# Loading the stacked per-batch factors ahead of the shared factors, and opening TensorE with three rounds of ones instead of nine

## The reference, cut to what matters

```
A_eff = einsum('bn,nri->bri', gate, lora_A)
B_eff = einsum('bn,nor->bor', gate, lora_B)
y     = x @ kernel + bias + (x @ A_eff[b].T) @ B_eff[b].T + (x @ lora_A_shared.T) @ lora_B_shared.T
```

## Time and profile before

| | |
|---|---|
| time of three runs | 492.47 us in the median, 491.3 to 493.65 |
| span of the profiled execution | 490.6 us |
| its own time on the device | not given beside the span; the median lies 1.87 us above the span |
| PE busy | 471.1 us (96%), 2168 matmuls |
| DVE busy | 408.6 us (83%) |
| ACT busy | 339.7 us (69%) |
| chain that ended last | PE 62%, DVE 26%, issue 7%, DMA 2%, ACT 2% |
| mean granted TensorE clock | 0.965 of full |

### The profile page before, as it was taken

One profiled execution on the slowest core, in us unless ns is written; L12 is line 12 of the kernel. 1 busy time (PEld: TensorE's weight loads), 2 busy tenths in 40 slices (PEclk: granted clock), 3 DMA queues, 4 the chain that ended last, 5 costly groups with the idle time before them and its releaser, 6 DMA issues.

```text
span 490.6 us, 5581 instructions
## 1 busy us (share of the span) xinstructions
PE 471.1 (96%) x2168; PEld 365.4 (74%) x2168; DVE 408.6 (83%) x411; ACT 339.7 (69%) x264; POOL 8.5 (2%) x12
## 2 busy tenths in 40 slices
PE   6989999999989999999999999999999989999796
PEld 5963888887758888787777777877787768767674
DVE  2289979779979989749899999999999994999402
ACT  3779987864978396676599596955977975583000
POOL 0000000001000000000000010000000000000000
PEclk9599999999999999999999999999999995999699
DMA  8975643212401527030523117104313130101102
GB/s 277 421 258 192 171 133 89 73 43 98 107 1 63 152 85 215 15 94 23 169 99 106 59 40 236 53 1 150 140 28 124 54 128 1 53 1 43 44 0 85
DMA packets 35499, 50.61 MB, mean 103 GB/s; under 512 B 26610, under 2 KB 26866, under 8 KB 33074
## 3 DMA queue, kind: packets, MB, share of 16 engines
q1 hardware_dynamic: 34322, 41.87, 26.6%
q0 software_dynamic: 1152, 8.39, 4.8%
HBM read 39.51 MB, written 10.49 MB: 102 GB/s over the span
## 4 chain that ended last, share of the span: by engine, by line
PE 62%; DVE 26%; issue 7%; DMA 2%; ACT 2%; SPq 0%; DVEq 0%; ACTq 0%
DVE val L593 12%; PE bank L949 7%; PE bank L951 7%; PE bank L950 7%; PE bank L837 6%; DVE val L576 5%; PE bank L906 5%; PE bank L902 5%; PE bank L903 4%; PE bank L931 3%; PE bank L863 3%; DVE inside L586 3%; PE bank L885 3%; PE bank L803 3%; DMA la<-la_in 2%
## 5 line engine op out<-in xcount | busy, mean ns | idle before, releaser
L403 ACT ACTIVATE val<-level,shift,small 128x2048 f32<-128x2048 int16 x64 | 133.8, 2090 | 22.5 <-DVE val L593 22.4
L593 DVE COPY_PREDICATED val<-inside,val 128x2048 f32<-128x2048 uint8 x56 | 142.1, 2538 | 0.3
L392 ACT ACTIVATE level<-xq,inv 128x2048 int16<-128x2048 f32 x64 | 127.9, 1998 | 2.2 <-DMA xq<-xt_in 1.4
L949 PE MATMUL bank<-p_hi,x_hi 128*128 128x512 f32 x256 | 113.1, 442 | 0.0
L951 PE MATMUL bank<-p_hi,x_lo 128*128 128x512 f32 x256 | 101.3, 396 | 0.0
L950 PE MATMUL bank<-p_lo,x_hi 128*128 128x512 f32 x256 | 101.2, 395 | 0.0
L576 DVE TENSOR_SCALAR val<-val,width,unshift 128x2048 f32<-128x2048 f32 x64 | 86.8, 1359 | 10.2 <-ACT val L403 10.0
L586 DVE TENSOR_SCALAR inside<-absx,thr 128x2048 uint8<-128x2048 f32 x56 | 72.1, 1297 | 6.1 <-ACT absx L384 6.1
L949 PEld LDWEIGHTS bank<-p_hi,x_hi 128*128 128x128 f32 x256 | 49.1, 192 | 18.9 <-issue 10.0
L950 PEld LDWEIGHTS bank<-p_lo,x_hi 128*128 128x128 f32 x256 | 48.9, 191 | 14.6 <-issue 5.8
L951 PEld LDWEIGHTS bank<-p_hi,x_lo 128*128 128x128 f32 x256 | 48.8, 191 | 10.8
(11 more groups left out here) (86 smaller groups left out, 454.3 us busy)
## 6 DMA issues: line engine op xcount, KB each, us to landing
xq<-xt_in POOLq DMA_DIRECT2D x8, 1024.0 KB, 6.1
xs<-xt_in SPq DMA_DIRECT2D x8, 1024.0 KB, 4.9
out_t<-ost SPq DMA_DIRECT2D x16, 512.0 KB, 3.0
wst<-w_in SPq DMA_DIRECT2D x14, 512.0 KB, 3.6
la<-la_in SPq DMA_DIRECT2D x4, 512.0 KB, 10.6
kst<-k_in SPq DMA_DIRECT2D x4, 512.0 KB, 14.0
lb<-lb_in SPq DMA_DIRECT2D x1, 2048.0 KB, 19.9
kst<-k_in SPq DMA_DIRECT2D x1, 2048.0 KB, 7.8
```

What stands on the lines that cost most here:

```text
L392: nc.scalar.activation(level[:, g % 2], xq[:, c % 2], ACT.Copy, scale=inv[:, g:g + 1]).then_inc(levels_made, 1)
L403: nc.scalar.activation(val[:, turn(c, g)], level[:, g % 2], ACT.Relu, bias=shift[:, g:g + 1], scale=par[:, 1, g:g + 1]).then_inc(raised, 1)
L593: nc.vector.copy_predicated(val[:, acc(c)], inside[:, g % 2], val[:, turn(c, g)]).then_inc(merged, 1)
L949: mm(o, x_hi[:, s, k, at], p_hi[:, h, k], start=k == 0, stop=False)
```

## The change

One constant and the place of one line. The rounds of ones ahead of the first products become three, and the load of the shared factors is issued behind the four parts of the stacked ones. The order on every other engine stays.

```diff
-WARM, WARMUPS = 256, 9
+WARM, WARMUPS = 256, 3
@@ block.sync
             sp.dma_start(small, a["small"]).then_inc(small_in, 16)
-            sp.dma_start(ab_raw, a["ab"]).then_inc(ab_in, 16)
             for g in range(NG):
                 sp.dma_start(la[:, g], a["la"][:, g]).then_inc(lora_in[g], 16)
+            sp.dma_start(ab_raw, a["ab"]).then_inc(ab_in, 16)
             sp.dma_start(bw, a["bw"]).then_inc(bw_in, 16)
```

## The result

The changed kernel takes 494.22 us in the median of twelve runs (492.53 to 497.23), the kernel before 492.29 in twelve beside it: a ratio of 1.0048, with a 95% interval from 1.0026 to 1.0069. That is slower, by 1.9 us between the medians and 2.4 us by the ratio, with an interval that leaves out 1. Forecast were 496.1 us and +3.6, so the time lies inside the stated range (493.4 to 499.0), 0.8 us above its near end. Of the profiled executions, the one after spans 492.2 us and took 493.97, the one before spans 490.6.

A forecast was written before the change was run, and what follows sets the result against it. An opening chain of waits (`la`, TensorE, ScalarE, VectorE, then L795) was taken to bound the kernel; ScalarE's +3.6 us, with TensorE's gain and the rounds at 0, gave span 494.2, plus 1.9 outside it: 496.1 us, range 493.4 to 499.0.

The forecast's parts named there:

- +3.6: Sum at VectorE's first mask and ScalarE's next work: 3.6 us later, carried to the end of the profiled span.
- `ab` lands last: SyncE's queue: behind the four `la` transfers `ab` lands at 14.8 us instead of 7.5, with 13.3 as near end.
- Rival A: Wait ahead of L478: `ab` lands before 11.2 us, kernel faster by up to 3.9 us, 488.6 us; chance 0.07.
- ScalarE carries it on: ScalarE's in-order work: evictions end 12.8 us after `ab` lands, at 27.6 instead of 24.0 us, +3.6 us.
- TensorE's gain is worth nothing: Products of `la` end 4.1 us earlier, at 19.3 us, but ScalarE takes the first bank only at 24.9.
- The rounds cost 0: TensorE's opening: three rounds for nine may slow the first products, but all lies under ScalarE's lateness; 0 us.
- up to 2 us: TensorE's products of `la`: cost of the missing rounds if ScalarE's lateness did not cover it.
- L795 at 39 to 40: TensorE's 16 products of L795 start at 39.7 us instead of 36.05, at 0.43 us a matmul.
- Rival B: TensorE's clock stays down into L795 after longer idleness, 6.9 us more, 503 us; chance 0.07.
- Rival C: Delay given back, by `ab` landing at 13.3 or earlier or a later stage absorbing it: 493.2 to 494.6 us; chance 0.18.
- shifted alike: Stages behind the opening: ScalarE, VectorE and TensorE all shift together, so the span goes from 490.6 to 494.2 us.

The follow-up runs named there:

- e1: Against the kernel before: only the load of `ab` moved behind `la`, nine rounds of ones kept; ratio 1.0061.
- e8: Against the changed kernel: ScalarE splits `ab` behind levels and values of groups 0 and 1, VectorE's remainders behind its values, nine rounds; ratio 0.9960 to the kernel before.
- e10: Against the changed kernel: the same late split of `ab` as e8, but with three rounds of ones; ratio 0.9960 to the kernel before.
- e9: The changed kernel measured again, nothing altered, beside the kernel before; ratio 1.0057, medians 3.06 us apart.
- e5: The kernel before measured again as a control, nothing altered; ratio 0.9991.
- e6: Against the kernel before: 10 and 14 unread filler products in TensorE's pauses ahead of the last two router products; 488.66 us, ratio 0.9926.
- e7: Against the changed kernel: the same 10 and 14 filler products in the same two pauses; 491.81 us, ratio 1.0012 to the kernel before.
- e11: Against e8 (late split, nine rounds): 10 and 22 filler products added in TensorE's two late pauses; 482.97 us, ratio 0.9832 to the kernel before.
- e2: Against the kernel before: only the rounds of ones cut from nine to three, `ab` still first; ratio 1.0016.
- e12: Against e11: a tiny copy at the head of ScalarE's program, so the table load runs early; 481.77 us, ratio 0.9796 to the kernel before.

## Why the prediction was right, point by point

- *`ab` lands last.* Forecast 14.8, measured 15.27 (15.1 to 16.1 over the eight profiles that have it behind all of `la` and ahead of `bw`). The reading of the backlog held: what stands ahead of a transfer in its queue sets its landing. Rival A, an overtaking `ab`, did not show in any profile: in the changed kernel the last `la` landed at 12.0, `ab` at 15.3 and `bw` at 16.2, in the order of issue. These landings agree with the half of the Trainium skill's "DMA: Bandwidth & Descriptors", "Queues, rings and completion order", on the order in which descriptors are consumed; no run here shows the other half, a later transfer that completes first.
- *ScalarE carries it on.* Forecast 12.8 us from landing to the end of the evictions, measured 12.1. Eight evictions back to back take 2.27 us and not 2.7: pairs of 0.66 us cannot be lined up, since the durations of neighbours overlap. The split, levels and values took 9.85 us for 10.1. The two errors, a landing 0.5 us later and a ScalarE 0.7 us shorter, nearly cancel, which is luck; the mask came at 29.25 for 29.6.
- *TensorE's gain is worth nothing.* Its products ended at 19.7 (forecast 19.3), 5.4 us ahead of the first eviction. e1 shows the worthlessness directly.
- *The rounds cost 0.* Right in result (e1 against the changed kernel, e8 against e10). One detail was wrong in the profiled run: the first 16 products ran at the full clock, 1.97 us for 16, at 5.3 us. In e9, the same kernel, they took 3.65 us (forecast 3.2 at half clock). The price without cover, "up to 2 us", is not shown: the opening moves by more than 1.4 us by itself.
- *L795 at 39 to 40.* 39.18. Rival B (slow L795) did not come: 6.87 us, although L813 took 5.75 us at 1.2 GHz for most of its length.
- *Rival C.* By its own sign (L795 3.6 us late and the span less than 2 us later) it nearly came about in the profiled pair: 3.29 and 1.6. The measured time of 494.22 lies in the band that the prediction gave to C (493.2 to 494.6). But neither of the reasons named for C holds: `ab` did not land by 13.3, and up to the seventh product no stage absorbs delay (369.2 to 369.5 us, always), nor does one between it and the eighth (45.0 to 45.2). The 1.8 us came back by the place where the clock falls in a router product, which the prediction did not have among its reasons, and e9 gives back nothing.
- *The size.* The forecast +3.6 was too large, and the 1.9 us between the medians are little more than half of it. Two terms of the sum were mis-sized. The opening gave +3.3 in the profiled pair, by the shorter ScalarE above. And the prediction carried the shift whole to the end of the kernel, "shifted alike", with no term for the granted clock near the end; in the profiled pair that term is -1.8. That is chance and not a property of the change, and the time fell inside the range in part because the range's near end took in most of C. The level of before that the shift is counted from moves too: L795 at 35.89 in one profile, and 35.03, 35.89 and 37.38 in the three profiles with that program's opening (before, e5, e6), 36.1 in the mean, while the changed opening hardly moves (39.18, 39.17, 39.32). Four measurements of the shift (1.9, 2.8, 3.1 and 3.15 us between the medians, 2.4, 3.0, 2.8 and 4.2 by the ratios, for the change, e1, e9 and the pair e6 and e7) lie around 3; the shift between the mean openings is 3.1. How much of the rest is the clock near the end and how much the opening of before is left open.

## What to carry to other kernels

Moving a load forward delays whatever it passes by the bytes now ahead of that, and an engine that works in order hands the delay to all that is queued behind the wait: before reordering loads, find on each engine the first instruction that waits for the load that loses, and move it too (e8 turned a loss of 0.5% into a gain of 0.4%). Where the time differs by less than the opening promises, compare the start of one late instruction in both kernels before looking for a stage that absorbs; here a distance of 369.4 us, the same within 0.3 us in fourteen profiles, settled it. Where one profiled pair disagrees with that, profile the same kernel again before explaining the difference (e9).

## What the runs showed of the hardware

- TensorE's pauses of 2.0 to 3.3 us ahead of the last two router products cost it the full clock in all ten profiles that leave them: the products took 3.8 us with their pauses filled and 4.8 to 7.1 without. A pause of 1.7 us, left in e6 and e7, still cost it (5.8 and 5.0 us). Filling both is worth about 6 of e11's 8.3 us (e10, without fillers, gained 2.3), more than the change under study.
- The clock column showed 1.00 from the start of a profile where the pace of the loads says 1.2 GHz (e2, 16 to 20 us), so a mean clock taken from such a profile is too high.
- The transfer of `ab`, 0.79 MB in 96 partitions, moved at 0.20 to 0.27 MB/us at a share of 0.9 to 1.0 wherever it stood in the queue (12 to 15 us in the changed kernel), against 0.41 MB/us for its neighbours.
- ScalarE's table load of 1.28 us sits ahead of its first activation. It ran at 0.74 us in the kernel before and in e12, ahead of the one wait in front of that activation, and at 8.8 us in e8, e10 and e11, where two waits stand in front of it. Why the wait held it there and not in the other two is not shown. A tiny copy put first hid it again (e12).
